# The head of a two-layer mixer: first chunk of x and base_w loaded first, base products from there on, DRAM arrays cut by chunk

## What is computed

```python
def L0_cond(x, e):                      # 64 batches, each with its own 32x32 mixing matrix
    h = gelu(gelu(e @ W0 + b0) @ W1 + b1)
    att = softmax(h @ W2 + b2)                       # 64 x 8
    agg_w = einsum('bk,koi->boi', att, weight)       # 64 x 32 x 32
    return einsum('boi,bih->boh', agg_w, x) + (att @ bias_k)[:, :, None]

def L0_ffn(x):                          # base product and 8 LoRA experts, the best 2 of them
    w = top2_softmax(x @ gate_w.T)
    return x @ base_w.T + base_b + 2 * sum_e w_e * (x @ A_e.T) @ B_e.T

x = x + L0_ffn(L0_cond(x, cond))
x = x + L1_ffn(L1_conv_and_context(x, cond, fside))  # 9 taps, 4 experts, the best 2 of them
```

## Time and profile before

| | |
|---|---|
| median of 3 executions | 176.72 us (175.42 to 178.06) |
| the profiled execution | 177.42 us |
| its span, first to last instruction | 175.7 us |
| TensorE busy, share of the span | 97% |
| VectorE, GpSimd, ScalarE busy | 71%, 54%, 50% |
| bytes moved | 13.21 MB, mean 75 GB/s |

### The profile page before, as it was taken

One profiled execution on the slowest core, in us unless ns is written; L12 is line 12 of the kernel. 1 busy time (PEld: TensorE's weight loads), 2 busy tenths in 40 slices (PEclk: granted clock), 3 DMA queues, 4 the chain that ended last, 5 costly groups with the idle time before them and its releaser, 6 DMA issues.

```text
span 175.7 us, 3106 instructions
## 1 busy us (share of the span) xinstructions
PE 169.9 (97%) x1098; PEld 159.1 (91%) x1098; DVE 125.4 (71%) x259; ACT 87.1 (50%) x204; POOL 94.2 (54%) x98
## 2 busy tenths in 40 slices
PE   7999999999999999999999999999999999999990
PEld 7878889999899999998899999999899999999880
DVE  6479199689963559998997336998997954367660
ACT  3864659886453477624251367332315463235231
POOL 8420507999199899936119199730006695066000
PEclk9999999999999999999999999999999999999999
DMA  5999500524001500000032000000041000000336
GB/s 176 237 332 393 202 0 0 194 69 164 14 0 60 168 16 0 4 0 0 0 134 111 0 0 0 4 2 0 15 167 60 0 0 4 2 0 0 122 121 239
DMA packets 7215, 13.21 MB, mean 75 GB/s; under 512 B 800, under 2 KB 1696, under 8 KB 7200
## 3 DMA queue, kind: packets, MB, share of 16 engines
q1 hardware_dynamic: 6768, 12.62, 21.1%
q10 hardware_dynamic: 432, 0.39, 0.7%
HBM read 8.82 MB, written 4.19 MB: 74 GB/s over the span
## 4 chain that ended last, share of the span: by engine, by line
PE 90%; DVE 4%; ACT 2%; issue 1%; POOL 0%; ACTq 0%; DVEq 0%; POOLq 0%
PE ps L1099 21%; PE ps L1101 20%; PE ps L1100 20%; PE ps L1191 8%; PE ps L1092 3%; PE ps L1112 3%; PE ps L1129 2%; PE ps L1288 2%; PE ps L1289 2%; DVE xsl L788 1%; PE ps L1172 1%; PE ps L1300 1%; DVE xs L920 1%; PE ps L1203 1%; PE ps L1330 1%
## 5 line engine op out<-in xcount | busy, mean ns | idle before, releaser
L1099 PE MATMUL ps<-xw_h,xTh 128*128 128x264 f32 (+1 forms) x96 | 30.6, 318 | 0.0
L1100 PE MATMUL ps<-xw_l,xTh 128*128 128x264 f32 (+1 forms) x96 | 29.9, 311 | 0.0
L1101 PE MATMUL ps<-xw_h,xTl 128*128 128x264 f32 (+1 forms) x96 | 29.8, 311 | 0.0
L371 POOL TENSOR_TENSOR xTl<-xT_s,xTh 128x512 fp32r<-128x512 f32 x12 | 15.7, 1333 | 21.1 <-ACT xTh L513 15.7
L376 POOL TENSOR_TENSOR zl<-outb,zh 128x340 fp32r<-128x340 f32 x15 | 15.1, 1007 | 14.9 <-ACT zh L548 7.9
L868 DVE TENSOR_TENSOR outb<-ps,s_sb 128x340 f32<-128x340 f32 x16 | 8.2, 510 | 14.5 <-PE ps L1101 10.8
L1099 PEld LDWEIGHTS ps<-xw_h,xTh 128*128 128x128 f32 x96 | 18.1, 188 | 0.3 <-issue 0.2
L1100 PEld LDWEIGHTS ps<-xw_l,xTh 128*128 128x128 f32 x96 | 18.1, 188 | 0.1
L1101 PEld LDWEIGHTS ps<-xw_h,xTl 128*128 128x128 f32 x96 | 18.1, 188 | 0.0
L1191 PEld LDWEIGHTS ps<-mixT,xp 128*128 128x128 f32 x128 | 16.7, 191 | 1.4 <-DVE x1T L855 0.2
L387 POOL TENSOR_TENSOR x1Tl<-x1T,x1Th 128x512 fp32r<-128x512 f32 x12 | 16.5, 1388 | 2.3 <-DVE late L892 2.3
(11 more groups left out here) (232 smaller groups left out, 519.2 us busy)
## 6 DMA issues: line engine op xcount, KB each, us to landing
xT_s<-in_xT_dram SPq DMA_DIRECT2D x16, 256.0 KB, 4.5
out_dram<-outb SPq DMA_DIRECT2D x12, 256.0 KB, 2.3
x1T<-in_wT_dram SPq DMA_DIRECT2D x4, 256.0 KB, 6.8
outb<-in_wrow_dram SPq DMA_DIRECT2D x4, 256.0 KB, 8.1
x1T<-in_az_dram SPq DMA_DIRECT2D x1, 680.0 KB, 9.4
outb<-in_tapw_dram SPq DMA_DIRECT2D x1, 576.0 KB, 3.8
out_dram<-x1T SPq DMA_DIRECT2D x2, 256.0 KB, 2.4
lgw_s<-in_lgw_dram SPq DMA_DIRECT2D x1, 272.0 KB, 3.4
```

The source lines that it names most:

```text
L371: nc.gpsimd.tensor_tensor(lo[:, c, :], xT_s[:, g % 2, c, :], hi[:, c, :].bitcast(F32), ALU.subtract).then_inc(x_lo, 1)
L1099: nc.tensor.matmul(dst, sh, mh, start=start and c == 0, stop=False)
L1100: nc.tensor.matmul(dst, sh, ml, start=False, stop=False)
L1101: last = nc.tensor.matmul(dst, sl, mh, start=False, stop=stop and c == n - 1)
```

## The change

Four things are changed.

- Sync loads chunk 0 of x and of base_w first, then early and lgw, then chunk 1, then a new array mixw, then chunks 2 and 3. mixw holds what was wrep and, behind it, the mixing bias that was in early. ScalarE issues no load at the start any more.
- TensorE's head: 20 filler products, then the base products of chunk 0, one tile at a time between the steps of the attention, where fillers stood; those of chunk 1 around the transposes of the attention; chunk 2 ahead of mix_logits(0), chunk 3 behind it. The first half of x_first(1) stands ahead of turn_lw(0). ScalarE and VectorE split the chunks in the matching order.
- GpSimd's low parts of group 1 don't wait for lb_lo any more.
- xT, wT, wrow and out are laid out in DRAM with the chunk ahead of the partition, so that a chunk is one contiguous piece of 256 KB; before, its rows of 2 KB lay 8 KB apart.

```diff
             def load_xT(g, c):
-                sp.dma_start(xT_s[:, g % 2, c, :], xT[g, :, c, :]).then_inc(xT_in[g % 2][c], 16)
-            sp.dma_start(early_s[:, :], early).then_inc(in_early, 16)
-            sp.dma_start(lgw_s[:, :, :], lgw).then_inc(in_lgw, 16)
+                sp.dma_start(xT_s[:, g % 2, c, :], xT[g, c, :, :]).then_inc(xT_in[g % 2][c], 16)
             for c in range(DC):
                 load_xT(0, c)
-                sp.dma_start(wT_s[:, c, :], wT[:, c, :]).then_inc(in_base[c], 16)
+                sp.dma_start(wT_s[:, c, :], wT[c, :, :]).then_inc(in_base[c], 16)
+                if c == 0:
+                    sp.dma_start(early_s[:, :], early).then_inc(in_early, 16)
+                    sp.dma_start(lgw_s[:, :, :], lgw).then_inc(in_lgw, 16)
+                elif c == 1:
+                    sp.dma_start(mixw_s[:, :], mixw).then_inc(in_mixw, 16)
...
             pool.wait_ge(base_lo, DC)
-            x_low(1, 0)
-            x_low(1, 1)
-            pool.wait_ge(lb_lo, 1)
-            x_low(1, 2)
-            x_low(1, 3)
+            for c in range(DC):
+                x_low(1, c)
...
         @block.scalar
-            act.dma_start(wrep_s[:, :, :], wrep).then_inc(in_wrep, 16)
...
-            keep_busy(4, 12)
+            keep_busy(4, 20)
+            x_base(0, 0, (0,))
...
-    xT = by_chunk(a["x"].reshape(G, TOK, D)).transpose(0, 4, 2, 3, 1).reshape(G, P, DC, TOK)
+    xT = by_chunk(a["x"].reshape(G, TOK, D)).transpose(0, 2, 3, 4, 1).reshape(G, DC, P, TOK)
```

More of the change, by code:

```diff
@@ L37, with two_layer_mixer @@
 SCALE1 = 16.0 / 16.0 ** 0.5
-A_COND, A_W0, A_W1, A_W2, A_B0, A_B1, A_B2, A_MB, A_N = 0, 64, 192, 320, 328, 329, 330, 338, 466
+A_COND, A_W0, A_W1, A_W2, A_B0, A_B1, A_B2, A_N = 0, 64, 192, 320, 328, 329, 330, 338
+M_W, M_B, M_N = 0, C * K0, C * K0 + P
 S_CTX, S_FS, S_BB, S_N = 0, 128, 129, 133
-def two_layer_mixer(nc: bass.Bass, xT, early, wrep, lgw, wT, wrow, lbT, az, tapw, b1T, side, out):
+def two_layer_mixer(nc: bass.Bass, xT, early, mixw, lgw, wT, wrow, lbT, az, tapw, b1T, side, out):
     with ExitStack() as ctx:
@@ L219, in two_layer_mixer @@
             sem(n) for n in ("consts", "const_step", "ident_ok", "out_act", "place_step", "place_ok", "warm_ok", "zero_ok"))
-        in_early, in_wrep, in_lgw, in_side, in_lb, in_az, in_tap, in_b1 = (
-            sem(f"in_{n}") for n in ("early", "wrep", "lgw", "side", "lb", "az", "tap", "b1"))
+        in_early, in_mixw, in_lgw, in_side, in_lb, in_az, in_tap, in_b1 = (
+            sem(f"in_{n}") for n in ("early", "mixw", "lgw", "side", "lb", "az", "tap", "b1"))
         in_base = [sem(f"in_base{c}") for c in range(DC)]
@@ L750, in _ @@
             act.wait_ge(last_act, 3)
[L751 removed]
+            act.dma_start(out[G - 1, 1, :, HALF:TOK], out_last[:, 1, HALF:TOK]).then_inc(last_odd, 16)
         @block.vector
@@ L1355, in _ @@
                              att_d[:, :, :].rearrange("b t k -> b (t k)"), start=True, stop=True).then_inc(attb_mm, 1)
-            keep_busy(4, 3)
-            for t in range(TG):
[L1358 to L1364, removed]
+            x_base(0, 2, (1,))
+            x_base(0, 3, (1,))
+            x_logits(1)
+            pe.wait_ge(attT_ok, 1)
+            pe.wait_ge(in_mixw, 16)
+            nc.tensor.matmul(mixb_b, mixw_s[0:K0, M_B:M_B + P], attT[:, :], start=True, stop=True).then_inc(mixb_mm, 1)
+            x_logits(2)
+            x_logits(3)
+            for t in range(TG):
+                x_base(0, t, (2,))
             pe.wait_ge(xl_ok, 2)
@@ L1370, in _ @@
                 mix_logits(0, t)
-            for c in range(2, DC):
-                for t in range(TG):
-                    x_base(0, t, (c,))
+            for t in range(TG):
+                x_base(0, t, (3,))
+            for t in range(TG):
+                x_first(1, t, (0, 1))
             turn_lw(0)
-            for chunks in ((0, 1), (2, 3)):
-                for t in range(TG):
-                    x_first(1, t, chunks)
+            for t in range(TG):
+                x_first(1, t, (2, 3))
             make_y(0)
```

82 lines of the change are left out of this document (44 added, 38 removed).

## The result

| | before | after |
|---|---|---|
| median of 16 executions | 176.15 us (175.06 to 178.06) | 178.11 us (176.84 to 179.33) |
| ratio, with its 95% interval | | 1.011 (1.008 to 1.0145) |
| the profiled execution, its span | 177.42, 175.7 us | 177.38, 175.7 us |

The change makes the kernel about 2 us slower. The 16 executions of the changed kernel stand in two groups of 8: at 176.84 to 177.9 us with a mean granted clock of 1.00, and at 178.3 to 179.3 us with 0.984 to 0.99. The profiled one belongs to the first.

The account below looks back on a forecast made before the run. TensorE, busy 97% of the span, was taken as the bound, with only its 12.7 us head able to give time. 2.1 us gained between the marks less 0.96 lost before them gives 1.1: 175.6 us, range 173.9 to 177.4.

Parts of the forecast that it names:

- M': Start of mix_logits(0) in the changed kernel: 22.05 us, from 21.05 plus 0.7 for a slow clock and 0.3 for waits.
- Y': Start of make_y(0) in the changed kernel, put at M' + 10.7 us, a distance 2.1 us shorter than before.
- the stall: TensorE's wait ahead of x_first(1) for the bank that p0_out empties; predicted as new, 0.6 us.
- Loads, chunk 0, the start: Head: x and base_w chunk 0 land in 3.8 and 4.6 us, are usable at 5.95; TensorE starts real work at 6.05.
- Rival (c): First loads come at the slow microsecond's pace, chunk 0 usable 3.2 us later: 178.8 us, up to 179.6; chance 0.07.
- rival (d): Head goes well, clock up within the fillers, chunks never late: M' = 21.05, gain 2.1, 174.6 us; chance 0.18.
- M: Mark on TensorE's chain where mix_logits of group 0 starts, 21.09 us in the profiled kernel before.
- Y: Mark where make_y(0) starts, 33.87 us in the profiled kernel before; behind it both programs have the same TensorE order.
- rival (a): VectorE or GpSimd takes over: GpSimd's low parts beside the gates delay them 0.5 to 1 us; 176.4 us; chance 0.17.
- GpSimd's low parts "there in time": Between M' and Y': group 1's low parts no longer wait for lb_l, so they are ready in time.
- The layout at nothing: Contiguous chunks in DRAM taken as worth nothing; at best chunks come at 400 GB/s from 4.6 us on.
- VectorE's slack behind Y: VectorE done at M' + 14.3, TensorE's mix_base(0, 2) at M' + 14.5: a slack of 0.2 us that just holds.

Follow-up runs that it names:

- e1: The changed kernel, with GpSimd starting the low parts of group 1's chunks 2 and 3 only after group 0's gates; median 176.38 us, ratio to before 1.001.
- before_again: The kernel before, unchanged, run again for a second trace; 175.35 us.
- before_again_2: The kernel before, unchanged, run once more on another chip; 175.23 us.
- e6: The changed kernel with 20 filler products in TensorE's wait ahead of x_first(1); median 177.08 us, ratio to before 1.009.
- e3: The kernel before with only xT, wT, wrow and out laid out by chunk in DRAM; median 175.10 us, ratio 0.998.
- e2: The changed kernel with the base products of chunk 2 behind mix_logits(0) again, GpSimd still not waiting; median 176.43 us, ratio to before 1.000.
- e4: The changed kernel with GpSimd waiting for the gates and chunk 2 behind mix_logits(0); median 175.28 us of eleven executions, one of 537.65 left out, ratio to before 0.995.

## Why the prediction was wrong

It gave 175.6 us (173.9 to 177.4), a gain of 1.1, and the changed kernel takes 178.1 against 176.15. The step that failed is the distance from M' to Y', with the stall in it at 0.6 us instead of 2.28; the mark for the comparison failed as well. Step by step:

- **Loads, chunk 0, the start: right.** Predicted landings 3.8, 4.6, about 5 and 6 to 7.9 us; 3.6, 4.2, 4.7 and 6.9 came. First base product 6.05 predicted, 5.82 came. Rival (c) is out. Two slips in the sums, on which nothing hung: the 20 fillers ended at 5.82 us, not 5.5, since 12 of them take 2.93 us and not 12 x 0.21; and the 2681 KB are counted with base_w chunk 3, not ahead of it.
- **M': near its floor.** Predicted 22.05 with 0.7 us for the clock and 0.3 for waits; M' was 20.76 to 21.02 in three traces, the 21.05 of rival (d). The clock rose at 5.6 to 6.4 us in them, not 7.5. In e1's trace, whose TensorE order is the same, it rose at 7.3 us and M is 21.27.
- **The mark it was compared with: wrong.** The prediction took M = 21.09 and Y = 33.87 from one execution and placed its gain beside the median. That execution is 2.1 to 2.2 us longer than before_again and before_again_2, because its clock rose at 12.7 us and theirs at 4.4 and 5.3. With the early rise M is 18.8 and Y 31.5; 22 of 35 executions take the time that goes with a Y of 31.5 to 32.4. The sum M' + 10.7 = 31.7 us, with the M' that came, would have met this 31.5: no gain at all, even if every step had held. The head that could give time had been shown by a late clock. Against an early one the first base product moves from 9.5 to 5.8 us, but with 12 base products (2.8 us) more ahead of it M is 2.2 us later; the 0.6 us between the two is what the predicted stall of 0.6 takes.
- **Y' - M' = 10.7: the step that failed.** It came to 12.53. The parts: base products of chunk 3 up to 24.87 us, 3.85 (3.7 predicted); the stall 2.28 (0.6 predicted); first half of x_first 3.04 (2.93); turn and second half 3.37 (3.37). 1.7 of the 1.8 us are the stall. The 0.6 was worked out from ScalarE's row with the gates at their old length; e1, with these lengths, shows 0.48. What was mis-sized is the price of GpSimd beside VectorE. The prediction named it, as rival (a), at 0.5 to 1 us and 0.17, and argued against it that the gates are short operations. They are, but a short operation that starts beside a long one here ends only behind it. Its other argument, that the stretched copy was the only case in the head, misread the trace. There was a second, in the same form as the stall: VectorE's low part of x chunk 1 took 1.19 us instead of 0.68 and ended at 11.76 us, 0.56 us behind the end of GpSimd's product for the bias rows (L359). In the trace of before, VectorE, then GpSimd:

```profile
10.57 1.19 DVE L788 TENSOR_TENSOR x1Tl<-xT_s,x1Th 128x512 fp32r<-128x512 f32 x1 [0.96 <-ACT x1Th L513]
```

```profile
10.16 1.04 POOL L359 TENSOR_TENSOR xs<-attT,early_s 8x512 f32<-8x512 f32 x1 [3.59 <-ACT attT L616]
```

And the copy (L942) was no mild stretch. It starts at 2.02 or 2.03 us in all 14 traces and takes 2.42 or 2.43 us in six of them, ending 0.08 us behind the second of two memsets of GpSimd, and 0.22 us in the other eight: held to the end or not at all, a price of 2.2 us and not of 0.5 to 1.
- **GpSimd's low parts "there in time": right, and costly.** e1 shows what the freedom was worth: a wait of 0.83 us at the second half of x_first.
- **What no case held: the clock's fall.** The stall makes TensorE idle, and in 8 of 16 executions, by their mean clock, the clock falls in it; in the two that were traced this costs another 1.3 us up to Y. e6 shows it by removing nothing but the idle time.
- **The layout at nothing: right for the time** (0.998, an interval with 1 in it), wrong for the loads, as e3 shows.
- **VectorE's slack behind Y: held.** The two operations behind the last mixing sum end at 37.20 us (36.45 + 0.75), TensorE's mix_base(0, 2) comes at 37.51, 3.8 us behind Y' as predicted. The slack of 0.2 is 0.3, since Y' moved along with the gates, and the time from Y to the end is as before, within 0.2 us.

The account of the loss, as far as shown: Y of before with an early rise 31.5, of the changed kernel 33.5 or 34.8. In the first case the stall beyond the 0.48 us of e1 is 1.8 of the 2.0 us. Undoing its cause (e1) or giving it cover (e2) takes 1.85 and 2.0 us back (1.0112 less 1.0007 and 0.9999, of 176 us), and both together (e4) 2.9. Only some of that is the stall: against the changed kernel's shorter eight executions e1 and e2 gain 0.5 us in the median, and their traces have Y at 33.15 and 33.47 for 33.55, e1 with its new wait of 0.83 us, and both with a clock that rises 1.6 us later. The rest is that the clock falls in none of their executions. The gains of e1 and e2 don't add up to that of e4, since both go for the same stall.

## What to carry to other kernels

Before a head is rebuilt, take several traces of it: the moment at which the clock rises moved this kernel's first base product by 1.5 us and its time by 2.2, and an edit that looked worth 1 us against the late one is worth nothing against the early one. When a wait is taken from an engine off the critical path, ask what will then run beside what: here two freed GpSimd operations fell on two VectorE operations that everything waited for. And a piece of work moved ahead of a mark is cover taken away behind it; the same held gates cost TensorE 0.55 us with two chunks behind mix_logits and 2.28 with one.

## What the runs showed of the hardware

- A VectorE operation with two inputs in SBUF that starts while a GpSimd operation runs ended a time behind GpSimd's end that went with its own size: 0.28 us for 256 columns (0.41 us became 1.14, 1.50 and 0.82), 0.55 us for 512 (0.68 us became 1.67 in e1). One with a single input, top, kept its 0.19 us beside the same GpSimd operation.
- VectorE's copy of place (L942 before), which starts at 2.02 or 2.03 us, took 0.22 us in eight traces and 2.42 in six, with the same GpSimd memsets beside it: held to their end, or not at all.
- With an idle time of 2.28 us on TensorE the granted clock fell for 3.4 us in two traces and not in a third, with the same order and the same idle time.
- Chunks of 256 KB in one piece instead of rows of 2 KB at 8 KB distance: 133 GB/s (41 to 133 in five traces) became 387 in the same microsecond, and base_w chunk 0 took 4.0 us instead of 5.7 (5.4 to 6.1).
